# Ten row buffers instead of four for the gathered rows of a graph network's second and third layer

## The reference

```python
# L0, three layers (gated graph network)
m   = x @ weight[l]
agg = jax.ops.segment_sum(m[src] * edge_weight[:, None], dst, num_segments=N)
x   = _gru_cell(agg, x, w_ih, w_hh, b_ih, b_hh)
# L1, three layers (graph isomorphism network)
agg = jax.ops.segment_sum(x[src], dst, num_segments=N)
x   = relu((x + agg) @ W.T + b)
# around them
x = _layernorm(x + L0(x));  x = _layernorm(x + L1(x))
```

## Time and profile before

| | |
|---|---|
| median of three runs | 3189.99 us (3188.34 to 3191.41) |
| the profiled execution | 3188.34 us, its span 3186.6 us |
| PE busy | 2949.5 us, 93% of the span |
| DVE busy | 1532.8 us, 48% |
| POOL busy | 974.1 us, 31% |
| rounds of the second gated layer | from 1118.18 us to about 1679 us of the span |
| rounds of the third gated layer | from 1734.38 us to about 2338 us |

### The profile page before, as it was taken

One profiled execution on the slowest core, in us unless ns is written; L12 is line 12 of the kernel. 1 busy time (PEld: TensorE's weight loads), 2 busy tenths in 40 slices (PEclk: granted clock), 3 DMA queues, 4 the chain that ended last, 5 costly groups with the idle time before them and its releaser, 6 DMA issues.

```text
span 3186.6 us, 75545 instructions
## 1 busy us (share of the span) xinstructions
PE 2949.5 (93%) x29405; PEld 1905.3 (60%) x29405; DVE 1532.8 (48%) x4507; ACT 902.3 (28%) x2115; POOL 974.1 (31%) x1214
## 2 busy tenths in 40 slices
PE   6999999999999999988868998777689999999998
PEld 5888888888888755444334544333355555555554
DVE  7888888888888334444442444344450001001111
ACT  5666666666666300000001010010130001001111
POOL 3232222222223155656551556556420000000000
PEclk8999999999999999989989999978889999999999
DMA  5665565565542698766765885855728786876884
GB/s 196 261 250 225 232 253 223 229 252 229 228 192 78 263 348 309 277 256 252 289 254 195 322 308 196 299 194 187 281 86 312 296 309 251 311 299 260 300 314 178
DMA packets 150125, 796.32 MB, mean 250 GB/s; under 512 B 19300, under 2 KB 29480, under 8 KB 136200
## 3 DMA queue, kind: packets, MB, share of 16 engines
q1 hardware_dynamic: 119960, 729.87, 59.1%
q0 software_dynamic: 27344, 54.53, 5.7%
q10 hardware_dynamic: 2720, 10.62, 0.8%
HBM read 567.97 MB, written 226.97 MB: 249 GB/s over the span
## 4 chain that ended last, share of the span: by engine, by line
PE 63%; DMA 15%; POOL 8%; DVE 6%; issue 6%; ACT 2%; another core or an unknown queue 0%; ACTq 0%; POOLq 0%; DVEq 0%
PE ps L1127 24%; PE ps L1206 18%; DMA ring<-y_rows,ring 15%; PE ps L1199 11%; POOL ring L836 7%; PE ps L923 4%; DVE ring L1738 4%; PE ps L1219 1%; PE ps L1220 1%; PE ps L1106 1%; PE ps L933 0%; ACT ring L1602 0%; PE ps L934 0%; DVE shared L1685 0%; DVE shared L1682 0%
## 5 line engine op out<-in xcount | busy, mean ns | idle before, releaser
L923 PE MATMUL ps<-ring,Y 128*128 128x448 f32 x2352 | 918.0, 549 | 57.7 <-issue 57.6
L836 POOL DMA_INDIRECT ring<-y_rows,ring x700 | 667.5, 954 | 592.3 <-DVE ring L1738 338.2
L1127 PE MATMUL ps<-ring,Y 128*128 128x448 f16 x4116 | 780.6, 352 | 0.0
L923 PEld LDWEIGHTS ps<-ring,Y 128*128 128x128 f32 x2352 | 453.4, 193 | 515.2 <-issue 515.2
L1602 ACT ACTIVATE ring<-ps 128x392 f16<-128x392 f32 (+1 forms) x1568 | 654.0, 506 | 303.2 <-PE ps L1199 296.8
L1738 DVE SCALAR_TENSOR_TENSOR ring<-ring 128x128 f32<-128x128 f32 x1384 | 417.4, 349 | 598.4 <-DMA ring<-y_rows,ring 551.0
L1127 PEld LDWEIGHTS ps<-ring,Y 128*128 128x128 f16 x4116 | 402.8, 98 | 373.8
L1206 PE MATMUL ps<-ring,Y 128*128 (+1 forms) x2744 | 613.9, 366 | 3.4 <-issue 2.9
L1206 PEld LDWEIGHTS ps<-ring,Y 128*128 128x128 f32 x2744 | 490.5, 189 | 19.3 <-issue 4.1
L1199 PEld LDWEIGHTS ps<-shared 64*128 64x128 bf16 x18816 | 340.6, 94 | 132.0 <-ACT ring L1602 87.0
L1199 PE MATMUL ps<-shared 64*128 64x49 bf16 (+1 forms) x18816 | 390.4, 190 | 22.1 <-issue 8.3
(11 more groups left out here) (188 smaller groups left out, 1331.1 us busy)
## 6 DMA issues: line engine op xcount, KB each, us to landing
ring<-adj_w SPq DMA_DIRECT2D x72, 2688.0 KB
adj_w<-ring SPq DMA_DIRECT2D x48, 2744.0 KB, 12.2
ring<-adj_h SPq DMA_DIRECT2D x42, 2800.0 KB
ring<-adj_h SPq DMA_DIRECT2D x42, 2688.0 KB, 9.2
adj_h<-ring SPq DMA_DIRECT2D x56, 1372.0 KB, 5.0
ring<-adj_w SPq DMA_DIRECT2D x24, 2912.0 KB
ring<-y_rows,ring POOLq DMA_INDIRECT x700
y_rows<-Y ACTq DMA_DIRECT2D x2, 2560.0 KB, 10.7
```

Of the source, the lines that this page charges most:

```text
L836: pool.indirect_dma_start(out=run_rows[:, i % ROW_BUFS, :], out_offset=None, in_=y_rows, in_offset=bass.IndirectOffsetOnAxis(ap=run_edges[ ...
L923: mm = pe.matmul(ps[:, bank, 0:GW], Y[:, h, :], slab(s)[:, :, h - h0, :], start=(h == 0), stop=(last and h == TILES - 1))
L1127: mm = pe.matmul(ps[:, par, 0:GW], part[:, h, :], counts_slab(par, s)[:, :, h - h0, :], start=(h == 0 and part is Y_high), stop=(h == TILE ...
```

## The change

`ROW_BUFS` is 10 instead of 4. It sizes the buffers in SBUF (six more of 128 fp32 elements a partition, and what lies behind them in `ring` moves by as much), the number of semaphores `s_row`, the buffer and semaphore of each round, and POOL's wait: a gather waits for the round ten before it instead of four. In the same places stand the same instructions on every engine; only buffers, semaphores and the values waited for differ.

```diff
@@ -40,7 +40,7 @@
 SH = 13
 RUN = 100
 RUN_SPANS = 4
-ROW_BUFS = 4
+ROW_BUFS = 10
 RUN_PAIRS = RUN_SPANS * 112
 RUN_LENGTHS = [RUN, RUN, RUN, RUN // 2]
 RUN_STARTS = [0, RUN, 2 * RUN, 3 * RUN]
```

## The result

With ten buffers the kernel took 3316.09 us (median of four runs, 3312.34 to 3317.65), against 3189.16 us for four buffers on the same chip (3181.37 to 3191.41): 1.0406 times as long, interval 1.039 to 1.0421. The prediction said 2961 us and named 2935 to 3070. It was wrong in size and in sign on this chip.

The account below looks back on a forecast made before the run. Too few buffers in the loop between POOL and DVE were taken as the bound. 3188.3 us less 100 in the second layer and 127 in the third gave 2961 us, range 2935 to 3070.

Parts of the forecast that it names:

- The loop of POOL and DVE: Gather issue, landing, DVE's add and back to POOL: 7.0 us for four rounds, 1.75 us a round with four buffers.
- POOL's waits for DVE: In the two gather layers, 1118 to 2340 us: to fall from 338 us to about 60 to 90.
- the stalls: POOL out of free buffers: about 7 us at mix 0, and 7 us at each statistics in the third layer.
- PE's pace is the other bound: PE in the groups, never idle: 41.34 us a group, just fitting POOL's 41.2 us for 33 rounds.
- The prediction's 50.7: Time a group with four buffers, second layer: 507.3 us from mix 0 to mix 10, over 10.
- PE's half-clock stretches after its idle times go: Unknown cost (b), more gathers beside PE's slab loads, downwards: PE's slow-clock stretches vanish, a gain up to 10 us.
- Rival C: Slower: gathers crowd the slab loads and PE waits for slabs; at 54 us a group 3268 us; chance 0.03.

Follow-up runs that it names:

- the short adds: Ten buffers, DVE's adds on 8 of 128 elements in every round but a run's first: 2931.7 us without phases, 3350.64 us on chip 3.

## Why the prediction was wrong

**What held.** The loop of POOL and DVE was the bound, and ten buffers open it. Where no phases come, every step is met. On chip 6 a group takes 41.3 us between mixes (1194.4, 1235.7, 1277.1). From the mix of group 0 to that of group 10 it is 404 us in the second layer (402 predicted) and 422 in the third (425). POOL starts 1.25 us apart, and the clock holds 1.00. The time is 2940 us where 2961 was said; 16.6 of these 21 us lie ahead of the first gather, which starts at 1101.6 us on that chip instead of 1118.2. POOL's waits for DVE were 131 us, not 60 to 90, but all but six of the 335 pieces are the 0.30 us that lie between two gathers at full pace anyway, 99 us together. What is left is six long waits: 6.4 and 6.7 us at mix 0 of the two layers, where I had said 7, and 4.9, 6.4, 3.5 and 3.3 us in the third layer, where I had said 7 each. So the stalls were the ones worked out, and those at the statistics smaller.

**What failed.** The step is the one that took PE's pace from the earlier trace rows and kept it: "PE's pace is the other bound", 41.34 us a group, beside gathers at 1.249, with the clock at 1.00. Each number was read where it was true. But 41.34 us was measured beside gathers 1.6 to 1.75 us apart, and 1.249 in stretches in which DMA was otherwise quiet. No row that I used showed both at once, for as long as the sum needed them. On this chip both at once last 26 to 30 us, and then a phase comes, in which PE issues one matmul in 2.1 to 2.8 us where it issued one in 0.376. The sum is 41.35 + 16 = 57.4 us a group from mix to mix, against 52.7 before. (The prediction's 50.7 takes in the step from group 9 to group 10, which is only 32.6 us long; like for like it is 52.7.) Of the 116 us by which mix 10 of the third layer is late, 26 are there at mix 0 of the second layer and 23 more come between the last mix of that layer and mix 0 of the third, both with the long first phase of a layer; the rest comes with the other groups.

**It stood in the trace of before.** This is PE of four buffers, right behind the eleven gathers of the earlier trace rows:

```profile
1344.46 17.83 PE L923 MATMUL ps<-ring,Y 128*128 128x448 f32 x47
1363.10 0.54 PE L923 MATMUL ps<-ring,Y 128*128 128x448 f32 x1 [0.81 <-issue]
1365.90 0.54 PE L923 MATMUL ps<-ring,Y 128*128 128x448 f32 x1 [2.26 <-issue]
1368.70 0.90 PE L923 MATMUL ps<-ring,Y 128*128 128x448 f32 x1 [2.27 <-issue]
```

and three of its windows:

```profile
1168.00:1333.00 165.00, 161.67 (x431) 81.41 (x429) 69.75 (x218) 7.99 (x14) 95.28 (x102) 1.00 0.85 312
1340.00:1360.00 20.00, 20.00 (x54) 10.15 (x53) 10.38 (x35) 1.16 (x2) 15.12 (x17) 0.99 0.21 53
1363.00:1383.00 20.00, 9.37 (x11) 2.72 (x11) 9.13 (x25) 0.58 (x1) 11.30 (x12) 0.62 0.38 126
```

102 gathers in 165 us (1.62 each) beside a PE busy for 162 of them: no phase. 17 gathers in 20 us, POOL's full pace, beside a full PE: a phase follows. The kernel before has five of these, each 25.5 to 26.8 us after the start of an unbroken run of 27 to 29 gathers; its other runs have at most 14 and bring none. I saw the half clock there and put it to PE's idle times, as "PE's half-clock stretches after its idle times go, up to 10 us": a gain. It was a sample of the cost. Of PE's 187 us of idle time in these two layers before, 58 were on "issue" and not waits for DVE, and the forecast gave them back with the rest. The five phases would have given a rival: if each group's 33 rounds at 1.25 us bring one, 20 to 24 phases of 16 us, 320 to 384 us on 2961. I had no such rival. Rival C had the sign and some of its size (54 us a group), but another mechanism, which did not occur.

**What is shown, and what is only likely.** Shown on chips 3, 10 and 15: slower gathers, with everything else kept, take the phases away step by step (20, 15, 2). On chip 10 the step from 20 to 2 was made side by side. Also shown: six buffers have them too, and an eighth of the bytes, a sixteenth of DVE's elements and half of PE's columns do not remove them. With PE's full columns a phase comes, but for a few, behind 20 to 26 gathers without a break, and at ten buffers and the full pace most end within 6 us of the last of them (within 10 with the short adds). That is when they come, not why; shorter runs of gathers, say 16 with a pause, would test it and were not run. Taking the gathers away left none, on a chip on which ten buffers were not run. Not shown: what inside the chip starts a phase or ends it, why 1.42 us is slow enough and 1.33 is not, whether a busy PE is needed at all, whether the placement of the arrays matters on these chips, and why chip 6 has none. That POOL keeps its 1.25 us through a phase, to the end of its run, while PE and DVE crawl together looks like something in the supply of instructions or semaphores rather than in the units; that is argued only.

## What to carry to other kernels

Two rates that were each measured while the other was low are not a rate for both at once; look for the stretch of the trace in which both are high, and read what comes right behind it. A wait on "issue" in front of an instruction that has nothing to wait for, with records of normal length but far apart, is a cost with a cause of its own: count such stretches in the kernel before, ask what brings them on, and multiply them by how often the change would bring it. Time a change of some per cent on more than one chip, since here the same edit gave 0.9335 and 1.04.

## What the runs showed of the hardware that was not expected

- Phases of 15 to 19 us (28 to 30 for the first of a layer) in which PE starts a matmul each 2.1 to 2.8 us mostly (normally 0.376) and DVE an instruction each 1.33 to 1.47 us, whatever their length (0.23 or 0.35 us). They come 25 to 31 us into a run of 128-row gathers by POOL 1.25 us apart, and mostly 30 to 34 us at 1.33, beside a full PE; with twice as many matmuls of half the columns, mostly 17 to 20 us.
- The granted clock falls within such a phase, to 0.61 in the mean of the one shown, and not before it (1.00 in the 25 us ahead). At half the columns the phases are about 31 us long (620 / 20), since they begin sooner in the run of gathers.
- Chips of one type differ: four buffers take 3150 us on chip 6 and 3184 to 3189 on the others. In 880 us of the first layer it is 19,064 matmuls against 18,673 to 18,725, with DVE's and ACT's instructions of the same mean length (765.93 / 2120 and 780.29 / 2160 are both 0.361 us; 594.43 / 1454 and 605.60 / 1481 both 0.409).
- A memset of 0.31 us ahead of a gather costs POOL 0.17 us (1.42 instead of 1.25), since it takes part of the 0.30 us between two gathers.
